# One scaling product for both heads, VectorE sums the pair and GpSimd adds the sum; fewer whole items; filling products in the last waits

## The chip, the cores and the metric

One Trainium2 chip, one of its cores. The metric is device microseconds of one execution; a figure with a range is a median of several. The profile is one execution with the hardware profiler on.

## The reference

Four batches of a 64 x 32 x 32 image pass three stages:

```python
# 1. attention over the 1024 pixels, 32 channels, no mask
q, k, v = wq @ x, wk @ x, wv @ x
x = x + wo @ (softmax(k.T @ q, axis=2) @ v.T).T
t = tokens(x)                                   # (4, 1024, 64)
# 2. causal attention, 8 heads of 64, on layernormed tokens
t = t + concat_h(softmax(mask(q_h @ k_h.T / 8)) @ v_h) @ Wo
# 3. a recurrence over the 1024 tokens, on layernormed tokens
w = batchnorm(layernorm(t) @ W.T) * gamma + beta
y[n] = sigmoid(w[n] + y[n-1] @ V.T);   t = t + y
```

Wo is folded into the value matrices of the heads, so each head's attention gives its own 64-column addend of the tokens.

## The kernel before

Every engine runs its own program; semaphores count finished steps. The middle of all programs is one loop over *slots*, numbered by items, in which each engine does its part of what is listed for that slot.

**Items.** The probabilities are made transposed, in items of 128 keys x 512 queries. The first attention has 64 items, one a slot. The second has 288, in 16 *units* (`v` from `B` on): a unit is one batch and two heads (`r` 0 and 1), nine items for each head, taken in pairs (item of head 0, item of head 1), so nine steps of two slots each. For a pair TensorE multiplies the masks into the banks, then three f16 products per head for the scores (`pe_score_masks`, `pe_scores`). ScalarE reads a bank twice (`act_item`): exponentials in f32 (L775), and again in f16 (L779). GpSimd subtracts the two for the low part (`pool_low`, L1250). Six slots (`LAG`), so three pairs, later TensorE multiplies values (`pe_values`) with f16 high and low parts, three products for each 128 queries (L574, L576, L578). A *whole* item has only the f32 exponentials, no second reading and no low part, and one f32 product for each 128 queries, which the trace shows as two records (L570). `whole(i)` names them: every `ATTN_WHOLE`-th of the 18 items of a unit, so with 6 the 6th, 12th and 18th (pairs 2, 5 and 8, head 1). Item 2's second run of two tiles is multiplied together with item 3.

**The maxima.** In the same slots TensorE computes rough scores of the next unit into two banks (`pe_maxes`, L497, with masks L483) and VectorE reduces each to row maxima (`dve_prep`, L903). TensorE's masks in a slot wait for both maxima of the pair before (`pe_wait_bank`). Each slot's work on TensorE is in this order: values, helpers (`pe_aux`: queries, values, keys), masks of the maxima, masks of the scores, maxima, scores. The masks of the scores wait until ScalarE is done with the first item of the pair before.

**The outputs.** A *half* is one head's output for 512 queries, 4 x 65 columns in a bank; its 65th column is the sum of the exponentials. The halves of head 0 lie in `OT[0]`, those of head 1 in `OT[1]`. The first 512 queries are closed by pair 2, the others by pair 8, each multiplied three pairs later. VectorE then, ahead of its other work in that slot, takes the reciprocals of the four 65th columns and multiplies (`dve_scale`, L979 and L983), into one of four buffers (`S_RING`), head 0 first. GpSimd adds each half to the tokens (`pool_add`, L1260), also ahead of its low parts in that slot. The next half of a head opens its bank only when the half before is scaled. There are 8 halves of the first attention and 64 of the second; the last one is added by VectorE (L1129).

**The tail.** After the loop come layernorm of the last batch (its first half of tokens already inside the loop, L1028 to L1068), transposes (L584), the product with W in two halves (L711), batchnorm statistics with an average over partitions (L715), and the solver: sweeps over four chunks, a product with V on TensorE and a sigmoid on ScalarE.

## Time and profile before

| | |
|---|---|
| median of 3 runs | 570.09 us (568.32 to 572.07) |
| the profiled execution | 568.85 us, span of the trace 567.0 us |
| mean granted TensorE clock | 0.974 |
| TensorE products busy | 490.0 us, 6771 |
| VectorE busy | 398.8 us, 909 |
| ScalarE busy | 429.3 us, 832 |
| GpSimd busy | 424.4 us, 463 |

The span runs from the first to the last instruction of the trace; the profiled execution's time has what lies around it as well. Busy times of TensorE are sums of records that overlap in its pipeline.

### The profile page before, as it was taken

What the parts mean: (1) busy time and instruction counts of PE and PEld (TensorE: products, weight loads), DVE (VectorE), ACT (ScalarE), POOL (GpSimd) and SP (SyncE); (2) the same over time, 40 slices, a digit from 0 to 9 for tenths busy, and PEclk for the clock granted to TensorE, in tenths of its full rate; (3) what the DMA queues carried; (4) which work ended last, traced back from release to release, by engine and by line L of the source; (5) the groups of instructions that cost most, each with busy time, mean ns of one, the idle gap of its engine ahead of it and who ended that gap; (6) DMA issues with size and microseconds to landing.
All of it is one profiled execution on the core that took longest, in us unless ns stands there. A gap on an engine that the chain in (4) does not pass through costs nothing.

```text
span 567.0 us, 16744 instructions
## 1 busy us (share of the span) xinstructions
PE 490.0 (86%) x6771; PEld 323.0 (57%) x6771; DVE 398.8 (70%) x909; ACT 429.3 (76%) x832; POOL 424.4 (75%) x463
## 2 busy tenths in 40 slices
PE   4699978988799998889999988998999999787783
PEld 1277655655565755565666756565666766564431
DVE  5878888767678786576767676766767786328757
ACT  3488867866778878587888878787888878785593
POOL 3867965857988797968788797899788799985002
PEclk9999999989999999799999999999999999998698
DMA  9100000000000000000000000000000000000001
GB/s 230 68 3 2 2 20 1 4 1 3 1 22 2 3 3 2 3 1 21 2 3 2 4 3 1 21 3 1 1 3 3 2 3 2 2 2 2 0 2 74
DMA packets 3580, 7.46 MB, mean 13 GB/s; under 512 B 1168, under 2 KB 1456, under 8 KB 3376
## 3 DMA queue, kind: packets, MB, share of 16 engines
q1 hardware_dynamic: 3056, 5.34, 3.5%
q8 instruction: 54, 0.88, 0.7%
q10 hardware_dynamic: 448, 1.05, 0.6%
q14 instruction: 22, 0.18, 0.1%
HBM read 4.22 MB, written 1.05 MB: 9 GB/s over the span
## 4 chain that ended last, share of the span: by engine, by line
PE 45%; DVE 22%; POOL 17%; ACT 9%; issue 6%; DMA 1%; DVEq 0%; SPq 0%; POOLq 0%; ACTq 0%
POOL probs_low L1250 10%; PE bank L537 9%; DVE attn_partial_max L903 7%; ACT probs_high L779 6%; PE bank L497 6%; PE bank L570 5%; PE bank L574 4%; DVE conv_partial_max L897 3%; PE bank L578 3%; PE bank L576 3%; PE bank L455 2%; PE bank L522 2%; PE bank L483 2%; PE bank L456 2%; POOL tokens L1260 2%
## 5 line engine op out<-in xcount | busy, mean ns | idle before, releaser
L1250 POOL TENSOR_TENSOR probs_low<-probs,probs_high 128x512 f16<-128x512 f32 x288 | 327.6, 1158 | 77.5 <-ACT probs_high L779 76.7
L775 ACT ACTIVATE probs<-bank 128x512 f32<-128x512 f32 x352 | 214.7, 611 | 84.2 <-PE bank L537 69.0
L903 DVE TENSOR_REDUCE attn_partial_max<-bank 128x1 f32<-128x512 f32 (+2 forms) x288 | 185.3, 685 | 99.5 <-PE bank L497 99.0
L779 ACT ACTIVATE probs_high<-bank 128x512 f16<-128x512 f32 x288 | 176.8, 614 | 0.0
L574 PEld LDWEIGHTS bank<-values_high,probs_high 128*128 128x128 f16 x1152 | 105.7, 98 | 74.2 <-issue 35.8
L574 PE MATMUL bank<-values_high,probs_high 128*128 128x65 f16 x1152 | 128.8, 196 | 15.5 <-POOL probs_low L1250 11.4
L576 PE MATMUL bank<-values_low,probs_high 128*128 128x64 f16 x1152 | 127.6, 194 | 0.0
L578 PE MATMUL bank<-values_high,probs_low 128*128 128x65 f16 x1152 | 127.1, 194 | 0.0
L576 PEld LDWEIGHTS bank<-values_low,probs_high 128*128 128x128 f16 x1152 | 106.9, 99 | 3.2
L578 PEld LDWEIGHTS bank<-values_high,probs_low 128*128 128x128 f16 x1152 | 107.2, 98 | 0.0
L570 PE MATMUL bank<-values,probs 128*128 128x65 f32 x512 | 71.7, 278 | 0.8 <-POOL probs_low L1250 0.8
L570 PEld LDWEIGHTS bank<-values,probs 128*128 128x128 f32 x512 | 64.7, 192 | 3.5 <-POOL probs_low L1250 1.0
L497 PE MATMUL bank<-attn_keys_high,queries_high 64*128 64x512 f16 (+3 forms) x384 | 56.7, 332 | 7.9 <-ACT probs_high L779 6.0
L1260 POOL TENSOR_TENSOR tokens<-scaled_outputs,tokens 128x256 f32<-128x256 f32 x71 | 51.7, 729 | 8.0 <-DVE scaled_outputs L983 3.3
L537 PE MATMUL bank<-queries_high,attn_keys_high 64*128 64x512 f16 (+3 forms) x384 | 55.6, 326 | 1.1 <-ACT probs_high L779 1.1
L537 PE MATMUL bank<-queries_high,attn_keys_low 64*128 64x512 f16 (+3 forms) x384 | 55.5, 325 | 0.0
L537 PE MATMUL bank<-queries_low,attn_keys_high 64*128 64x512 f16 (+3 forms) x384 | 55.5, 325 | 0.0
L897 DVE TENSOR_REDUCE conv_partial_max<-bank 128x1 f32<-128x512 f32 x64 | 42.8, 687 | 5.8 <-PE bank L470 4.7
L983 DVE TENSOR_TENSOR scaled_outputs<-bank,reciprocal_denominators 128x256 f32<-128x256 f32 x72 | 30.6, 425 | 7.6 <-DVE reciprocal_denominators L979 0.5
L522 PE MATMUL bank<-causal_masks,identity_bf 128*128 128x128 bf16 x256 | 27.5, 219 | 6.6 <-ACT probs_high L779 6.4
L497 PEld LDWEIGHTS bank<-attn_keys_high,queries_high 64*128 64x128 f16 x384 | 15.3, 93 | 29.7 <-issue 6.8
L1343 POOL TENSOR_TENSOR x_split<-probs 128x512 f32<-128x512 f32 x4 | 4.2, 1092 | 36.1 <-ACT probs L878 36.1
(192 smaller groups left out, 708.9 us busy)
## 6 DMA issues: line engine op xcount, KB each, us to landing
x_channels<-in_x_cm SPq DMA_DIRECT2D x6, 256.0 KB, 7.6
tokens<-in_x_tm SPq DMA_DIRECT2D x1, 1024.0 KB, 10.4
out<-ln_channels SPq DMA_DIRECT2D x4, 256.0 KB, 2.0
attn_weights<-in_attn_w ACTq DMA_DIRECT2D x1, 512.0 KB, 6.2
attn_keys_split<-attn_keys_high SPq DMA_DIRECT2D x4, 128.0 KB, 2.3
attn_keys_split<-attn_keys_low SPq DMA_DIRECT2D x4, 128.0 KB, 2.4
queries_high<-minus_max_rows SPq DMA_DIRECT2D x32, 2.0 KB
x_channels<-in_x_cm ACTq DMA_DIRECT2D x2, 128.0 KB, 3.2
```

Source lines behind the costliest of these rows:

```text
L497: last[r] = nc.tensor.matmul(prep_bank(m + r)[:, at * P:(at + tiles) * P], q[rows(r), t * P:(t + 1) * P], xs_hi[rows(r), b * N + j0 * P:b ...
L537: last[r] = nc.tensor.matmul(ST[(i + r) % ST_RING][:, at * P:(at + tiles) * P], keys[rows(r), b * N + j * P:b * N + (j + 1) * P], queries[ ...
L570: ins = nc.tensor.matmul(dst, e32[:, item % E_RING, cols], v32[v % 2][:, j, r, :], start=opens, stop=True, skip_group_check=True)
L574: nc.tensor.matmul(dst, hi, v_hi[v % 2][:, j, r, :], start=opens, stop=False, skip_group_check=True)
L576: nc.tensor.matmul(dst[:, 0:C], hi, v_lo[v % 2][:, j, r, :], start=False, stop=False, skip_group_check=True)
L578: ins = nc.tensor.matmul(dst, lo, v_hi[v % 2][:, j, r, :], start=False, stop=True, skip_group_check=True)
L775: ins = nc.scalar.activation(e32[:, i % E_RING, :], o[:], ACT.Exp, scale=scale)
L779: ins = nc.scalar.activation(p_hi[:, i % P_RING, :], o[:], ACT.Exp, scale=scale)
L897: nc.vector.reduce_max(cmx[v % 2][:, t, part:part + 1], o[:], AX).then_inc(s_prep_used, 1)
L903: nc.vector.reduce_max(dst, o[:].rearrange("p (n w) -> p n w", n=n), AX).then_inc(s_prep_used, 1)
L1250: nc.gpsimd.tensor_tensor(out=p_lo[:, i % P_RING, :], in0=e32[:, i % E_RING, :], in1=p_hi[:, i % P_RING, :], op=ALU.subtract).then_inc(s_r ...
L1260: nc.gpsimd.tensor_tensor(out=dst, in0=scaled[:, half % S_RING, :, :], in1=dst, op=ALU.add).then_inc(s_added, 1)
```

## The change

- The reciprocals of both heads are taken in one instruction and both outputs are scaled in one product (`dve_scale_pair`), for which the two output banks become one tensor. It waits until both heads' values are closed. VectorE then sums the two scaled outputs, and GpSimd adds the sum to the tokens: one add for a pair, not two. The last pair is added by VectorE.
- `ATTN_WHOLE` goes from 6 to 9, so the whole items of a unit are the 9th and the 18th: head 0 of pair 4, and head 1 of pair 8.
- `pe_keep_clock` puts bf16 products of 256 columns into a bank that nobody reads, in five places behind the loop: 8, 6, 22, 3 and 18 of them.

```diff
-CONV_WHOLE, ATTN_WHOLE = 4, 6
+CONV_WHOLE, ATTN_WHOLE = 4, 9
+def added_by(half):
+    return half + 1 if half < B * NC else B * NC + (half - B * NC) // 2 + 1
-        banks = [ctx.enter_context(nc.psum_tensor(f"bank{i}", [P, CW], f32)) for i in range(8)]
-        ST, MX, OT, AUX = banks[0:3], banks[3:5], banks[5:7], banks[7]
+        banks = [ctx.enter_context(nc.psum_tensor(f"bank{i}", [P, CW], f32)) for i in range(6)]
+        both = ctx.enter_context(nc.psum_tensor("output_banks", [P, 2, CW], f32))
+        ST, MX, OT, AUX = banks[0:3], banks[3:5], (both[:, 0, :], both[:, 1, :]), banks[5]
+        def pe_keep_clock(bank, n):
+            for _ in range(n):
+                nc.tensor.matmul(bank[:, 0:2 * P], identbf[:], masks[:].rearrange("p a c -> p (a c)"),
+                                 start=True, stop=True)
...
             pe.wait_ge(s_l3t, 2)
+            pe_keep_clock(MX[0], 8)
             pe.wait_ge(s_l3, 3)
             pe_transposes(MX[1], xh3, 2).then_inc(s_tr, 1)
+            pe_keep_clock(MX[0], 6)
             pe.wait_ge(s_trc, 1)
             nc.tensor.matmul(ST[0][:], ffn_w[:, 0, :], xh3T[:, 2 * CW:3 * CW], start=True, stop=True).then_inc(s_wxp, 1)
+            pe_keep_clock(MX[0], 22)
             for t in range(TPC):
                 pe.wait_ge(s_l3, 4 + t)
...
             pe.wait_ge(s_aux_used, len(AUXES))
+            pe_keep_clock(ST[1], 3)
...
             pe.wait_ge(s_bn3, 1)
             pe.wait_ge(s_t2c, 2)
+            pe_keep_clock(MX[0], 18)
...
+        def dve_scale_pair(half):
+            nc.vector.wait_ge(s_values, CLOSED_BY[half + 1][3] + 1)
+            i = half % S_RING
+            po = both[:, :, 0:TPC * PO].rearrange("p r (t c) -> p r t c", c=PO)
+            nc.vector.reciprocal(rden[:, i:i + 2, :], po[:, :, :, C:PO].rearrange("p r t c -> p r (t c)")) \
+                .then_inc(s_recip, 2)
+            if half >= S_RING:
+                nc.vector.wait_ge(s_added, added_by(half - S_RING))
+            nc.vector.wait_ge(s_recip, half + 2)
+            nc.vector.tensor_tensor(out=scaled[:, i:i + 2, :, :], in0=po[:, :, :, 0:C],
+                                    in1=rden[:, i:i + 2, :].unsqueeze(3).to_broadcast([P, 2, TPC, C]),
+                                    op=ALU.mult).then_inc(s_scaled, 2)
+            nc.vector.wait_ge(s_scaled, half + 2)
+            nc.vector.tensor_tensor(out=scaled[:, i, :, :], in0=scaled[:, i, :, :], in1=scaled[:, i + 1, :, :],
+                                    op=ALU.add).then_inc(s_paired, 1)
...
                 for half in HALVES_AT.get(g, ()):
-                    dve_scale(half)
+                    if half < B * NC:
+                        dve_scale(half)
+                    elif half % 2 == 0:
+                        dve_scale_pair(half)
...
-            dve.wait_ge(s_added, HALVES - 1)
-            dve.wait_ge(s_scaled, HALVES)
+            dve.wait_ge(s_added, added_by(HALVES - 3))
+            dve.wait_ge(s_paired, (HALVES - B * NC) // 2)
...
-            nc.gpsimd.wait_ge(s_scaled, half + 1)
+            if half < B * NC:
+                nc.gpsimd.wait_ge(s_scaled, half + 1)
+            else:
+                nc.gpsimd.wait_ge(s_paired, (half - B * NC) // 2 + 1)
...
-                    if half < HALVES - 1:
+                    if half < B * NC or half % 2 == 0 and half < HALVES - 2:
                         pool_add(half)
```

## Rows read from the trace of the kernel before

**Rows 1.** The page, its part 4: shares of the chain that ended last.

```profile
PE 45%; DVE 22%; POOL 17%; ACT 9%; issue 6%; DMA 1%; DVEq 0%; SPq 0%; POOLq 0%; ACTq 0%
```

**Rows 2.** Stretches: length, busy time (count) by engine, clock, DMA share, GB/s.

```profile
421.71:445.40 23.69, 22.55 (x356) 15.42 (x356) 17.39 (x40) 19.85 (x39) 19.84 (x20) 1.00 0.01 3
470.00:500.00 30.00, 25.75 (x414) 17.88 (x410) 12.80 (x28) 23.66 (x48) 27.66 (x37) 1.00 0.01 2
524.00:526.00 2.00, 0.33 (x2) 0.18 (x1) 1.73 (x10) 0.60 (x1) 0.00 (x0) 0.50 0.01 4
```

**Rows 3.** Groups by line: busy us, mean ns, idle before and its releaser.

```profile
L1250 POOL TENSOR_TENSOR probs_low<-probs,probs_high 128x512 f16<-128x512 f32 x288 | 327.6, 1158 | 77.5 <-ACT probs_high L779 76.7
...
L1260 POOL TENSOR_TENSOR tokens<-scaled_outputs,tokens 128x256 f32<-128x256 f32 x71 | 51.7, 729 | 8.0 <-DVE scaled_outputs L983 3.3 <-POOL tokens L1260 0.4
...
L983 DVE TENSOR_TENSOR scaled_outputs<-bank,reciprocal_denominators 128x256 f32<-128x256 f32 x72 | 30.6, 425 | 7.6 <-DVE reciprocal_denominators L979 0.5
...
L964 DVE TENSOR_TENSOR queries_low<-bank,queries_high 128x512 f16<-128x512 f32 x32 | 21.8, 681 | 0.0
```

**Rows 4.** Timeline of ScalarE, slot 4: start, length, instruction.

```profile
434.74 0.64 ACT L775 ACTIVATE probs<-bank 128x512 f32<-128x512 f32 x1
435.22 0.65 ACT L779 ACTIVATE probs_high<-bank 128x512 f16<-128x512 f32 x1
```

**Rows 5.** The chain in order of time, slot 6: start, us, what.

```profile
437.62 0.47 PE bank L570 x4
...
438.42 0.03 PE bank L578
438.45 0.26 PE bank L483 x2
```

**Rows 6.** Timeline of VectorE, slots 4 and 5 of the unit.

```profile
435.18 0.68 DVE L964 TENSOR_TENSOR queries_low<-bank,queries_high 128x512 f16<-128x512 f32 x1
435.78 0.17 DVE L979 RECIPROCAL reciprocal_denominators<-bank 128x4 f32<-128x4 f32 x1
436.06 0.42 DVE L983 TENSOR_TENSOR scaled_outputs<-bank,reciprocal_denominators 128x256 f32<-128x256 f32 x1
...
437.01 1.28 DVE L903 TENSOR_REDUCE attn_partial_max<-bank 128x1 f32<-128x512 f32 x2
```

**Rows 7.** Timeline of VectorE, layernorm of the last batch and the last sum.

```profile
513.71 1.08 DVE L988 TENSOR_SCALAR ln_rstd<-ln_var_eps 128x4 int32<-128x4 int32 x1
...
517.05 1.08 DVE L996 SCALAR_TENSOR_TENSOR ln_rstd<-ln_newton_scratch,ln_rstd 128x4 f32<-128x4 f32 x1
518.16 0.17 DVE L994 TENSOR_TENSOR ln_newton_scratch<-ln_rstd,ln_var_eps 128x4 f32<-128x4 f32 x1
...
521.71 0.42 DVE L1129 TENSOR_TENSOR tokens<-scaled_outputs,tokens 128x256 f32<-128x256 f32 x1 [0.22 <-POOL tokens L1260]
```

**Rows 8.** Timeline of GpSimd, the same stretch.

```profile
511.37 6.73 POOL L1250 TENSOR_TENSOR probs_low<-probs,probs_high 128x512 f16<-128x512 f32 x6
```

**Rows 9.** Timeline of GpSimd, slots 3 to 5 of the unit.

```profile
433.50 2.27 POOL L1250 TENSOR_TENSOR probs_low<-probs,probs_high 128x512 f16<-128x512 f32 x2 [0.24 <-ACT probs_high L779]
435.95 2.28 POOL L1250 TENSOR_TENSOR probs_low<-probs,probs_high 128x512 f16<-128x512 f32 x2 [0.17 <-ACT probs_high L779]
```

**Rows 10.** Timeline of VectorE, first reciprocals of slot 5, first and last of 11.

```profile
155.86 0.17 DVE L979 RECIPROCAL reciprocal_denominators<-bank 128x4 f32<-128x4 f32 x1
...
459.84 0.17 DVE L979 RECIPROCAL reciprocal_denominators<-bank 128x4 f32<-128x4 f32 x1
```

**Rows 11.** Timeline of TensorE: one f32 product in the loop, the others in the tail.

```profile
398.29 1.12 PE L660 MATMUL bank<-ln_channels,ffn_weights 128*128 128x512 f32 x2 [0.49 <-DVE values_low L959]
...
522.08 2.07 PE L702 MATMUL bank<-ln_channels,ffn_weights 128*128 128x512 f32 x2 [0.69 <-ACT ln_channels L845]
525.82 1.14 PE L584 MATMUL bank<-constants,ln_tokens 128*128 128x128 f32 x4 [1.67 <-DVE ln_tokens L1135]
527.08 2.04 PE L711 MATMUL bank<-ln_channels,ffn_weights 128*128 128x256 f32 x4
```

More of the change, by code:

```diff
@@ L370, in build @@
         s_scaled = sem("outputs_scaled")
+        s_paired = sem("outputs_of_both_heads_added")
         s_added = sem("outputs_added")
@@ L980, in dve_scale @@
             if half >= S_RING:
-                nc.vector.wait_ge(s_added, half - S_RING + 1)
+                nc.vector.wait_ge(s_added, added_by(half - S_RING))
             nc.vector.wait_ge(s_recip, half + 1)
@@ L1017, in dve_ln3_tile @@
             if first:
-                nc.vector.wait_ge(s_added, (B + (b + 1) * H) * NC)
+                nc.vector.wait_ge(s_added, added_by((B + (b + 1) * H) * NC - 1))
             link(nc.vector.bn_stats(stats3[:, t, :], tok[:, (t * B + b) * C:(t * B + b + 1) * C]))
@@ L1060, in dve_norms @@
             if g == LAST_STATS_SLOT:
-                nc.vector.wait_ge(s_added, half_of(UNITS - 1, 0, 1) + 1)
+                nc.vector.wait_ge(s_added, added_by(half_of(UNITS - 1, 0, 1)))
                 last_stats(0)
@@ L1123, in _ @@
                 dve_norms(g)
-            dve.wait_ge(s_added, HALVES - 1)
-            dve.wait_ge(s_scaled, HALVES)
+            dve.wait_ge(s_added, added_by(HALVES - 3))
+            dve.wait_ge(s_paired, (HALVES - B * NC) // 2)
             dst = tok3[:, TPC:NT, (B - 1) * C:B * C]
-            link(nc.vector.tensor_tensor(out=dst, in0=scaled[:, (HALVES - 1) % S_RING, :, :], in1=dst, op=ALU.add))
+            link(nc.vector.tensor_tensor(out=dst, in0=scaled[:, (HALVES - 2) % S_RING, :, :], in1=dst, op=ALU.add))
             last_stats(1)
@@ L1255, in pool_add @@
             b = batch_of(v)
-            nc.gpsimd.wait_ge(s_scaled, half + 1)
+            if half < B * NC:
+                nc.gpsimd.wait_ge(s_scaled, half + 1)
+            else:
+                nc.gpsimd.wait_ge(s_paired, (half - B * NC) // 2 + 1)
             if half:
-                nc.gpsimd.wait_ge(s_added, half)
+                nc.gpsimd.wait_ge(s_added, added_by(half) - 1)
             dst = tok3[:, c * TPC:(c + 1) * TPC, b * C:(b + 1) * C]
@@ L1333, in _ @@
                     if g == slot + 8:
-                        pool.wait_ge(s_added, (B + (2 + n) * H) * NC)
+                        pool.wait_ge(s_added, added_by((B + (2 + n) * H) * NC - 1))
                 for k in range(NC):
```

## The prediction

> **What bounds the kernel now.** I read the shares of the chain that ended last first, then the groups by cost, then one repeating stretch engine by engine. In the chain no engine leads alone: TensorE has 45% of the span, VectorE 22%, GpSimd 17%, ScalarE 9% [rows 1]. So a saving on one engine is worth nothing until I know who ends the wait in each slot.
>
> The second attention repeats a unit (a batch and two heads) of nine slots of two items each, and from 421.71 to 445.40 us one takes 23.69 us. In it GpSimd is busy 19.84 us and VectorE 17.39; TensorE shows 22.55, but its records overlap, so that is no measure of it [rows 2]. In other stretches GpSimd is the bound: 27.66 us of 30 from 470 to 500 us [rows 2]. The clock is 1.00 in both; in the tail it is at 0.50, the lower of the two levels (1.2 GHz), from 524 to 526 us [rows 2].
>
> I number a unit's slots 0 to 8. The half of the output that closes first in a unit is scaled in slot 5, the other in slot 2 of the next unit.
>
> **GpSimd's work.** Removed: 32 of its 71 adds (39 are left), at 729 ns, 23.3 us. Added: 16 low parts at 1158 ns, 18.5 us, since "whole" items go from 48 to 32 of 288 [rows 3]. Net 4.8 us less in all, 0.3 us a unit. That counts only where GpSimd is the bound, about four units' worth of the run: 1.3 us. Against it stands the new sum of VectorE, below; I take nothing for the two together.
>
> **ScalarE's work.** 16 more exponentials. Two in a row start 0.48 us apart (434.74, 435.22) [rows 4], so 7.7 us in all, mostly in second items of slots 2 and 5, behind which ScalarE waits for scores anyway. In slot 4 the first item becomes whole, which frees the scores of slot 5 by up to 0.48 us. Whether that is worth anything is settled by VectorE (below).
>
> **TensorE's work.** The chain gives 0.47 us for four f32 value products (half of an item's eight), so 0.94 for a whole item, and 0.03 for each f16 product, so 0.36 for a split item's twelve [rows 5]. Each item that is split saves 0.58 us: 9.3 us over 16. But by place it is not a plain saving: per unit slot 8 loses one whole item (0.58 less), slot 7 gains one (0.58 more), and slots 5 and 6 each lose half of one. Slots 7 and 8 are near TensorE's bound both, so they nearly cancel. I take +0.1 us a unit, 1.5 us for 15 units; the bounds are one such item either way, -0.58 and +0.58 us a unit, since either can be hidden while the other is not.
>
> **VectorE's work.** This is the step that decides. Before, two reciprocals and two products run from 435.78 to 437.01, when the first maximum of slot 5 starts: 1.23 us [rows 6]. After: one reciprocal (0.28 to the product's start, 435.78 to 436.06 [rows 6]), one product over 512 columns (681 ns by the 512-column product that reads a bank, L964 [rows 3]), and a sum of two SBUF tiles over 256 columns (0.42 us by the last sum, L1129 [rows 7], of which 0.34 are seen by an instruction that does not need its result: half of the 1.23, less the reciprocal's 0.28). With 0.04 between, 0.28 + 0.68 + 0.04 + 0.34 = 1.34 us, 0.1 more than before.
>
> The sum has a second cost. VectorE instructions on four columns with their inputs in SBUF, 0.17 us when GpSimd is idle (518.16), took 1.08 us four times in a row, from 513.71 to 517.05 [rows 7]. GpSimd meanwhile ran six low parts without a gap from 511.37, 6.73 us, or 1.12 each [rows 8]. The third border lies at 514.74 and the last part ends at 518.10; the first and the fourth of those instructions end at 514.79 and 518.13. So each waited until GpSimd's current instruction was over. The products that read a bank kept their 425 ns on average [rows 3] while GpSimd was busy beside them. The new sum reads two SBUF tiles: it should wait likewise, and then hold GpSimd for up to its own 0.34 us.
>
> The Trainium skill says the same of wider operands (SBUF — State Buffer, section "Who interferes with whom"): a VectorE instruction with two SBUF inputs contends with a GpSimd instruction that reads SBUF, and whoever starts first keeps the other out for its whole length. It speaks against this change; no row here shows a two-input sum of 256 columns beside GpSimd. By that page the wait is the rest of GpSimd's instruction, as I take it; without the page's rule and the small rows the sum would cost 0.1 us.
>
> How long is the wait? In slot 5 the sum is ready at 435.78 + 1.00 = 436.78. GpSimd's turn there: before, it starts a low part at 433.50 and one at 435.95 [rows 9]. After, slot 2's second item gives one low part more, so I work the queue forward at 1.13 us each: slot 3's two end at about 436.3, slot 4's only one starts at about 436.35 (its exponential ends then: 434.74 + 3 x 0.48 plus a semaphore) and ends at 437.5. The sum gets in at 437.5, and slot 5's first maximum starts at about 437.85 instead of 437.01: **0.8 us later**. The bounds are 0.1 us (no wait) and 1.2 (a whole low part and 0.1).
>
> Who is late next? TensorE's masks of slot 6 start at 438.45 right behind the value products [rows 5], and they also wait for both maxima of slot 5, which end at 437.01 + 1.28 = 438.29 [rows 6]. So VectorE is level with TensorE now, and what it is late, slot 6 is late. The earlier scores of slot 5 do not help: VectorE runs without a gap into slot 5, no row from the low queries at 435.18 on has idle time before it [rows 6], and TensorE's shorter values in slot 6 are finished before. What is queued behind the sum on VectorE is the maxima, the row maxima, and layernorm tiles; on GpSimd, the add of the pair waits for the sum, and behind it slot 5's low parts, for which the values come due three slots later, so they have the room.
>
> In how many units? In 11 of the 15 that prepare another, the reciprocal of this half starts without any idle time before it, from 155.86 to 459.84 [rows 10]. Two of them (at 331 and 384 us) lie where the chain, read in pieces of 10 us, is mostly GpSimd's, as such a stretch shows in [rows 2]. Nine units by 0.8 us: **7.2 us**. In slot 2 the sum is ready about 0.3 us before a border, and VectorE has 0.4 us to spare behind it: nothing, but for the slots where the keys of the next batch are transposed; 0.5 us for all. A unit that is longer gives GpSimd time to work off what the layernorms left: I take off 1.0 us.
>
> **The tail.** The last pair is scaled and summed on VectorE with GpSimd idle: 0.1 us more, but the wait for GpSimd's add ahead of the last sum, 0.22 us [rows 7], goes. Nothing. The filling products (57 of 256 columns) are to keep the clock. At 0.50 the f32 product took 2.07 us for two records of 512 columns, at 1.00 1.12 us [rows 11]. On the chain lie the last transposes, 1.14 us, and the Wx products in two halves, 2.04 us [rows 11]; the first half's is covered in part by statistics that VectorE still runs. I give the transposes 0.3, the Wx products 0.8 and the averages 0.1: **1.2 us saved**. The product at 522.08 is off the chain: its result is needed 2 us later. The fillers cost nothing if they end inside the wait: 22 of them at 0.11 us are 2.4 us, between the end of a fast product (about 523.2) and the tokens at 525.6. If the clock were low they would take 0.21 us each, 4.6 from 524.15 on, and end 3 us after the tokens: bounds -1.6 and +3 us. The solver's first sweep at the low clock hides behind ScalarE's sigmoids.
>
> **The sum.** 7.2 + 1.5 + 0.5 - 1.0 - 1.2 + 0 = +7.0 us on the profiled execution's 568.85 (span 567.0 and 1.85 around it), so 575.9; the median of the runs is 1.24 above it, so **577 us**.
>
> **Rivals.**
> *A. The sum does not wait for GpSimd.* The small instructions at 513.71 and after are of another size, and a sum of 256 columns may get in otherwise, or arrive between two low parts. Then slot 6 is late by 0.1 us: 0.9 + 1.5 - 1.2 and 1.3 less for GpSimd's stretches is -0.1: 570 us. For it: no row of this width beside GpSimd. Against: four of four.
> *B. TensorE's saving is on the path and VectorE's lateness is not: faster.* Values are products right behind each other in the chain, and slot 8 is one that TensorE ends. If in 12 units its 0.58 us counts, and slot 7's cost falls in the wait for ScalarE there, the gain is 7.0; with 1.2 from the tail and 1.3 from GpSimd's stretches, 560.6 us. It decides if the pair's sum ends less than about 0.1 us later than the second product does now. Against it stands that VectorE is level already.
> *C. Full price.* The queue moves so that the sum always just misses: 1.2 us x 11, 1.5 and 0.5 us as above, and the tail's fillers at the low clock, +3: 588 us.
> *D. The fillers do not hold the clock* while the rest is as forecast: 577 + 1.2 + 3 = 581 us; inside the range.
>
> **How the numbers follow.** Forecast with D 0.47, A 0.28, B 0.16, C 0.09. The forecast's own range is 572 to 582 (nine units at 0.4 to 1.2 us). The range that should hold 8 in 10 takes in A with its tail bound and part of C: 564 to 585. A change under 1%, 5.7 us, can hardly be told from none here. Slower by over 1%: most of the forecast's cases and C, 0.52. Within 1%: A, the low part of the forecast and of B, 0.31. Faster: 0.17.
>
> **What would show it.** Right: the line of the pair's sum on VectorE with a mean well over 425 ns, often ending where a low part ends; its first maximum in slot 5 later after the reciprocal than 1.23 us; masks waiting for the maxima; units of 24.3 us or more; the clock at 1.00 between 520 and 530 us. Wrong: the sum at 425 ns (A), units under 23.5 us (B), or the masks of slot 6 still released by TensorE's own values, in which case VectorE had room that I did not see.

## The result and the profile after

The changed kernel took **583.6 us**, median of 4 runs (582.11 to 586.57), against 570.31 us for the kernel before on the same chip (568.32 to 572.07): 1.0241 times as long, with a 95% interval of 1.0188 to 1.0293. The profiled execution took 583.34 us, its span is 581.5 us (567.0 before), its mean granted clock 0.979 (0.974 before). The forecast was 577 us in a range of 564 to 585. So the direction and the range held, and the size of the change, +7, was about half of what was measured, +13.3.

The shares of the chain that ended last, to be held against [rows 1]:

```profile
PE 37%; DVE 31%; POOL 15%; ACT 11%; issue 5%; DMA 0%; DVEq 0%; SPq 0%; POOLq 0%; ACTq 0%
```

VectorE has gone from 22% of the span to 31%, TensorE from 45% to 37%. By stretches, with the columns of [rows 2] (a whole unit, the stretch from 470 us, and 2 us of the tail):

```profile
436.42:461.86 25.44, 21.80 (x361) 14.90 (x361) 19.65 (x40) 20.24 (x41) 19.56 (x18) 1.00 0.01 2
470.00:500.00 30.00, 25.55 (x413) 16.90 (x411) 21.92 (x42) 23.39 (x46) 25.58 (x36) 1.00 0.01 3
...
534.00:554.00 20.00, 17.85 (x119) 11.27 (x119) 17.24 (x68) 9.79 (x19) 0.00 (x0) 1.00 0.00 1
```

A steady unit takes 25.44 us, where it took 23.69. VectorE's busy time in it rose by 2.26 us (17.39 to 19.65) though it has one instruction to the pair less; 0.4 us of that is one more layernorm tile that happens to lie in this stretch. The groups by line show where that sits (columns as in [rows 3]):

```profile
L1008 DVE TENSOR_TENSOR scaled_outputs<-scaled_outputs 128x256 f32<-128x256 f32 x32 | 28.7, 897 | 1.1
L1302 POOL TENSOR_TENSOR tokens<-scaled_outputs,tokens 128x256 f32<-128x256 f32 x39 | 28.2, 724 | 8.7 <-DVE scaled_outputs L1008 8.4 <-DVE scaled_outputs L1019 0.3
...
L1004 DVE TENSOR_TENSOR scaled_outputs<-output_banks,reciprocal_denominators 128x512 f32<-128x512 f32 x32 | 22.1, 692 | 4.3
```

The sum of the pair (L1008) shows 897 ns on average, while the same form of instruction, 256 columns from two SBUF tiles, took 0.42 us in [rows 7] with GpSimd idle. The product of 512 columns (L1004) is at 692 ns, as forecast from L964 in [rows 3]. GpSimd is less busy than before, 420.2 us of the span against 424.4, and from 470 to 500 us 25.58 against 27.66 [rows 2], though that stretch now holds somewhat earlier work: it isn't what became the bound.

Who waits for VectorE's maxima now (the view of waits of the kernel after, where L497 is the masks and L511 the rough scores; the columns are us in all, times, longest):

```profile
PEld bank L497 <- DVE attn_partial_max L922: 18.6, 30, 1.4
PE bank L497 <- DVE attn_partial_max L922: 15.2, 28, 1.3
PEld bank L511 <- DVE attn_partial_max L922: 14.2, 14, 1.4
```

The same view of the kernel before, where L483 is the masks and L497 the rough scores:

```profile
PEld bank L497 <- DVE attn_partial_max L903: 6.7, 13, 0.7
...
PE bank L483 <- DVE attn_partial_max L903: 1.4, 6, 0.4
```

Products and weight loads overlap, so the rows of an engine's two parts aren't to be added; but the masks' wait went from 1.4 us to 15.2, and that of the rough scores' weights from 6.7 to 14.2 in about as many places (13 and 14), at most 1.4 us each instead of 0.7.

**By slots.** The start of ScalarE's first exponential of a pair marks the slot. The distances between these starts in one steady unit, and the sum of their differences over units 1 to 15, worked out from ScalarE's timeline (the distance to slot n is put down to slot n; 421.71 is the start of a slot 8 and 436.42 of a slot 0, so both stretches are nine slots long):

```
slot                      0     1     2     3     4     5     6     7     8   unit
before, from 421.71      2.51  2.88  2.95  2.29  2.40  2.26  2.71  2.43  3.26  23.69
after, from 436.42       2.57  2.87  2.96  3.18  2.40  1.95  3.81  2.82  2.88  25.44
units 1 to 15, after
  less before            (0, 1, 2, 4 together +0.7)
                                         +10.0       -3.6  +9.6  +5.7  -7.3
```

Slots 5 and 6 together are +6.0, slots 7 and 8 together -1.6. Unit 0 gives -1.2 and the work ahead of it +0.7. That is +14.8 until the last pair starts (515.05 before, 529.80 after), and the rest of the span is 0.25 us shorter. So two places pay: slot 6, where the sum of slot 5 is in the way, and slot 3, behind the sum of slot 2.

**Slot 5**, as forecast. VectorE's timeline of the kernel after, to be held against [rows 6]:

```profile
423.44 0.20 DVE L999 RECIPROCAL reciprocal_denominators<-output_banks 128x8 f32<-128x8 f32 x1
423.77 0.69 DVE L1004 TENSOR_TENSOR scaled_outputs<-output_banks,reciprocal_denominators 128x512 f32<-128x512 f32 x1
424.50 1.04 DVE L1008 TENSOR_TENSOR scaled_outputs<-scaled_outputs 128x256 f32<-128x256 f32 x1
425.46 1.28 DVE L922 TENSOR_REDUCE attn_partial_max<-bank 128x1 f32<-128x512 f32 x2
```

GpSimd's, to be held against [rows 9]:

```profile
424.10 1.16 POOL L1289 TENSOR_TENSOR probs_low<-probs,probs_high 128x512 f16<-128x512 f32 x1 [0.67 <-ACT probs_high L798]
```

And TensorE's, the masks of slot 6:

```profile
426.88 0.27 PE L497 MATMUL bank<-causal_masks,identity_bf 128*128 128x128 bf16 x2 [1.02 <-DVE attn_partial_max L922]
```

The low part occupies GpSimd from 424.10 to 425.26, and the sum, started at 424.50, ends 0.28 us after it. The first maximum follows 2.02 us after the reciprocal (forecast 2.07; 1.23 before). TensorE's masks of slot 6 come behind the maxima, after 1.02 us of idle time.

**Slot 2**, not as forecast. VectorE's timeline of the kernel after, 17 us later:

```profile
440.58 0.21 DVE L999 RECIPROCAL reciprocal_denominators<-output_banks 128x8 f32<-128x8 f32 x1 [0.23 <-PE output_banks L584]
440.93 0.69 DVE L1004 TENSOR_TENSOR scaled_outputs<-output_banks,reciprocal_denominators 128x512 f32<-128x512 f32 x1
441.65 1.42 DVE L1008 TENSOR_TENSOR scaled_outputs<-scaled_outputs 128x256 f32<-128x256 f32 x1
443.00 1.28 DVE L922 TENSOR_REDUCE attn_partial_max<-bank 128x1 f32<-128x512 f32 x2
```

GpSimd's:

```profile
440.52 2.27 POOL L1289 TENSOR_TENSOR probs_low<-probs,probs_high 128x512 f16<-128x512 f32 x2 [0.67 <-ACT probs_high L798]
```

And TensorE's weight load of the rough scores of slot 3:

```profile
444.34 0.12 PEld L511 LDWEIGHTS bank<-attn_keys_high,queries_high 64*128 64x128 f16 x2 [1.41 <-DVE attn_partial_max L922]
```

GpSimd runs two low parts without a gap from 440.52 to 442.79; the border between them lies near 441.65. The sum is ready at 441.65, does not get in there, and takes 1.42 us, 1.0 us more than its own work of 0.42: nearly a whole low part. The weight load comes 0.06 us behind the maxima. For comparison the same place on VectorE in the kernel before:

```profile
428.07 0.17 DVE L979 RECIPROCAL reciprocal_denominators<-bank 128x4 f32<-128x4 f32 x1
...
429.40 1.29 DVE L903 TENSOR_REDUCE attn_partial_max<-bank 128x1 f32<-128x512 f32 x2
```

and on ScalarE, the second exponential of slot 2:

```profile
430.55 0.59 ACT L779 ACTIVATE probs_high<-bank 128x512 f16<-128x512 f32 x1
```

Measured from the first exponential of slot 2 (430.05 before, 442.25 after, so 12.20 us apart) the maxima start 1.40 us later: 443.00 - 12.20 = 430.80 against 429.40. Before, they had room: the rough scores of slot 3 waited for the exponential that ends at 431.14, 0.45 us after the maxima do (430.69). Of the 1.40 us, 0.95 are left, and slot 3 is 0.89 longer (2.29 to 3.18). The sums of slot 2 are longer than 0.5 us in 12 of 15 units, 1.01 us on average: 1.42 us in five units, 1.14 in three, 0.68 to 0.91 in four, and 0.42 or 0.43 in the other three. So to just miss a border, as here, is the dearest case but not the only one; in seven units the sum is ready somewhere in the middle of a low part and waits for the rest of it.

**The tail.** VectorE, to be held against [rows 7]:

```profile
532.36 1.08 DVE L1030 TENSOR_TENSOR ln_newton_scratch<-ln_rstd,ln_var_eps 128x4 f32<-128x4 f32 x1
533.47 0.17 DVE L1031 SCALAR_TENSOR_TENSOR ln_newton_scratch<-ln_newton_scratch,ln_rstd 128x4 f32<-128x4 f32 x1
...
536.35 0.42 DVE L1008 TENSOR_TENSOR scaled_outputs<-scaled_outputs 128x256 f32<-128x256 f32 x1
536.88 0.42 DVE L1168 TENSOR_TENSOR tokens<-scaled_outputs,tokens 128x256 f32<-128x256 f32 x1
```

TensorE, to be held against [rows 11]:

```profile
536.92 1.13 PE L718 MATMUL bank<-ln_channels,ffn_weights 128*128 128x512 f32 x2
537.88 2.56 PE L460 MATMUL bank<-causal_masks,identity_bf 128*128 128x256 bf16 x22
540.99 0.55 PE L598 MATMUL bank<-constants,ln_tokens 128*128 128x128 f32 x2 [0.54 <-DVE ln_tokens L1174]
```

With GpSimd idle from 533.42 on, the last sum takes 0.42 us and the small instructions fall from 1.08 to 0.17. The 22 filling products end at 540.44, 0.55 us before the transposes are ready, and the clock is 1.00 from 534 to 554 us where it was 0.50 from 524 to 526 [rows 2]. From the last sum of tokens to the first sigmoid of the solver it is 10.48 us (536.88 to 547.36), before 11.79 (521.71 to 533.50).

### The profile page after: what moved, and what is told of

Same layout as the page of the kernel before. It is cut to its first block, busy times and chain, and to the rows that moved or that the text cites. A ratio compares the mean times of both kernels' runs of the same rounds, so it can differ in the third digit from the quotient of the medians.

```text
span 581.5 us, 16912 instructions
## 1 busy us (share of the span) xinstructions
PE 482.5 (83%) x6892; PEld 316.9 (54%) x6892; DVE 424.4 (73%) x877; ACT 436.0 (75%) x848; POOL 420.2 (72%) x447
## 4 chain that ended last, share of the span: by engine, by line
PE 37%; DVE 31%; POOL 15%; ACT 11%; issue 5%; DMA 0%; DVEq 0%; SPq 0%; POOLq 0%; ACTq 0%
DVE attn_partial_max L922 10%; POOL probs_low L1289 10%; PE bank L551 7%; ACT probs_high L798 5%; PE bank L511 5%; PE output_banks L584 4%; DVE conv_partial_max L916 3%; PE output_banks L588 3%; ACT probs L794 3%; DVE scaled_outputs L1008 3%; DVE scaled_outputs L1004 2%; PE output_banks L592 2%; PE bank L469 2%; PE output_banks L590 2%; DVE queries_low L983 2%
## 5 line engine op out<-in xcount | busy, mean ns | idle before, releaser
L588 PEld LDWEIGHTS output_banks<-values_high,probs_high 128*128 128x128 f16 x1216 | 111.7, 98 | 71.4 <-POOL probs_low L1289 35.6
L588 PE MATMUL output_banks<-values_high,probs_high 128*128 128x65 f16 x1216 | 133.1, 196 | 18.8 <-POOL probs_low L1289 9.4
L590 PE MATMUL output_banks<-values_low,probs_high 128*128 128x64 f16 x1216 | 132.1, 194 | 0.0
L592 PE MATMUL output_banks<-values_high,probs_low 128*128 128x65 f16 x1216 | 131.7, 194 | 0.0
L590 PEld LDWEIGHTS output_banks<-values_low,probs_high 128*128 128x128 f16 x1216 | 112.6, 99 | 3.5 <-issue 0.6
L592 PEld LDWEIGHTS output_banks<-values_high,probs_low 128*128 128x128 f16 x1216 | 112.8, 98 | 0.0
L511 PE MATMUL bank<-attn_keys_high,queries_high 64*128 64x512 f16 (+3 forms) x376 | 56.6, 331 | 12.5 <-ACT probs_high L798 8.6
L584 PEld LDWEIGHTS output_banks<-values,probs 128*128 128x128 f32 x384 | 47.6, 191 | 9.2 <-issue 6.8
L584 PE MATMUL output_banks<-values,probs 128*128 128x65 f32 x384 | 51.4, 277 | 0.0
L497 PE MATMUL bank<-causal_masks,identity_bf 128*128 128x128 bf16 x251 | 27.0, 218 | 15.2 <-DVE attn_partial_max L922 15.2
L536 PE MATMUL bank<-causal_masks,identity_bf 128*128 128x128 bf16 x256 | 27.4, 219 | 9.5 <-ACT probs_high L798 9.5
L1302 POOL TENSOR_TENSOR tokens<-scaled_outputs,tokens 128x256 f32<-128x256 f32 x39 | 28.2, 724 | 8.7 <-DVE scaled_outputs L1008 8.4
L511 PEld LDWEIGHTS bank<-attn_keys_high,queries_high 64*128 64x128 f16 x376 | 15.3, 93 | 33.3 <-DVE attn_partial_max L922 14.2
```

Source lines behind the costliest of these rows:

```text
L511: last[r] = nc.tensor.matmul(prep_bank(m + r)[:, at * P:(at + tiles) * P], q[rows(r), t * P:(t + 1) * P], xs_hi[rows(r), b * N + j0 * P:b ...
L584: ins = nc.tensor.matmul(dst, e32[:, item % E_RING, cols], v32[v % 2][:, j, r, :], start=opens, stop=True, skip_group_check=True)
L588: nc.tensor.matmul(dst, hi, v_hi[v % 2][:, j, r, :], start=opens, stop=False, skip_group_check=True)
L590: nc.tensor.matmul(dst[:, 0:C], hi, v_lo[v % 2][:, j, r, :], start=False, stop=False, skip_group_check=True)
L592: ins = nc.tensor.matmul(dst, lo, v_hi[v % 2][:, j, r, :], start=False, stop=True, skip_group_check=True)
L1302: nc.gpsimd.tensor_tensor(out=dst, in0=scaled[:, half % S_RING, :, :], in1=dst, op=ALU.add).then_inc(s_added, 1)
```

## The experiments

Each ratio is that to the kernel before, run on the same chip, with its 95% interval.

**e1, the pair without the other two parts.** The kernel after with

```diff
-CONV_WHOLE, ATTN_WHOLE = 4, 9
+CONV_WHOLE, ATTN_WHOLE = 4, 6
-            pe_keep_clock(...)      # all five calls
...
```

> The change with ATTN_WHOLE back at 6 and without the filling products: one product for both heads, the sum on VectorE, one add on GpSimd. Theory (the sum of two SBUF tiles waits for the low part that GpSimd has in hand, in slot 2 for a whole one, in slot 5 for a part of one, and the maxima behind it come late): 578 to 586 us, the sum's line at 750 ns or more on average, no gain from the whole items. Rival W (the shift of the whole items and their f32 products on TensorE is what costs): at most 572 us. Rival J (it is the waiting for both heads and the joint product, not the sum): 578 us or more too, but with the sum at 425 ns.

Measured: 581.83 us, 1.0209 (1.0184 to 1.0235). The pair alone gives nearly the whole loss, and the sum's line shows 869 ns, which speaks for the sum and against the mere joint product. In a steady unit slots 3 and 6 are 3.18 and 3.01 us instead of 2.29 and 2.71, the others as before.

**e2, the whole items alone.** The kernel before with `ATTN_WHOLE` 9.

> The kernel before with ATTN_WHOLE at 9 and nothing else: 16 more low parts on GpSimd with all 71 adds. Theory: TensorE saves in slot 8 what it loses in slot 7, GpSimd has 18 us more to do and is the bound in more places: 570 to 577 us. Rival W: 578 us or more.

Measured: 573.84 us, 1.0072 (1.0045 to 1.0099), +4.1 us. The shares of its chain:

```profile
PE 36%; POOL 24%; DVE 23%; ACT 11%; issue 5%; DMA 1%; DVEq 0%; POOLq 0%; SPq 0%; ACTq 0%
```

and of its waits that of GpSimd for ScalarE:

```profile
POOL probs_low L1250 <- ACT probs_high L779: 65.5, 69, 2.6
```

GpSimd's part of the chain goes from 17% to 24% and it waits 65.5 us for ScalarE where it waited 76.7 [rows 3]. So sixteen low parts more, without the adds saved, do cost: GpSimd gets near the bound.

**e3, the filling products alone.** The kernel before with the 57 products in the same five places.

> The kernel before with the 57 filling products of the tail and nothing else. Forecast of the prediction: 1.2 us less, 568.9 us, with the clock at 1.00 from the last values to the first sweep; 1.31 us less from the last sum of tokens to the first sigmoid, if the trace of the changed kernel is a guide. Rival: they delay what is behind them, 570.1 us or more.

Measured: 567.79 us, 0.9972 (0.9952 to 0.9992): -1.6 us. The three parts measured alone, 2.09 + 0.72 - 0.28 = 2.53%, agree with the 2.41% of the whole change, so there is no large share that only their combination makes.

**e4, one product for both heads and no sum.** The kernel before with `dve_scale_pair` up to the product and both scaled outputs added by GpSimd as before:

```diff
+            nc.vector.wait_ge(s_values, CLOSED_BY[half + 1][3] + 1)
...
+            nc.vector.reciprocal(rden[:, i:i + 2, :], ...).then_inc(s_recip, 2)
...
+            nc.vector.tensor_tensor(out=scaled[:, i:i + 2, :, :], in0=po[:, :, :, 0:C], ...,
+                                    op=ALU.mult).then_inc(s_scaled, 2)
```

> The kernel before with one reciprocal and one product for both heads, and no sum: GpSimd adds each head's output as before. Theory: the two-input sum is what costs, so this stays within 2 us of before: 568 to 572 us. Rival J (the joint product, its wait for both heads and the later opening of the banks): 575 us or more.

Measured: 569.59 us, 1.0002 (0.9985 to 1.0019). The common wait for both heads, the common reciprocal and the product of 512 columns cost nothing together. What is left of e1 is the sum.

**e5 and e6, VectorE time with two and with one SBUF input.** The kernel before, with one instruction more behind the second product of each pair; nobody reads its result:

```diff
+            if half >= B * NC and half % 2:
+                nc.vector.tensor_tensor(out=spare[:], in0=cst[:, 0:256], in1=cst[:, 256:512], op=ALU.add)   # e5
+                nc.vector.reduce_max(spare[:, 0:1], cst[:, 0:256], AX)                                    # e6
...
+            dve.wait_ge(s_cst, 16)                                                                    # both
```

The last line makes VectorE wait for the constants before its first cast of the run. That starts at 6.86 us (e6) and 6.70 us (e5), in the kernel before at 2.81, and ScalarE's first exponential comes at 25.43 and 25.07 us, where it comes at 22.67 in the kernel before and between 21.5 and 23.6 in all other kernels here.

> The kernel before, and behind each pair's second product a sum of two constant SBUF tiles of 256 columns that nobody reads. Theory (it waits for GpSimd): its line well over 425 ns on average, 550 or more, and 574 to 582 us. Rival (VectorE's own time is the cost, no wait): 425 ns and the time of the kernel with a maximum in its place.

> As the one before, with a maximum over one SBUF tile of 256 columns in the place of the sum: the same time on VectorE, one SBUF input. Theory: no wait, a line of some 425 ns, 571 to 575 us, and less than with the sum.

Measured: e5 587.44 us, 1.0300 (1.0262 to 1.0338); e6 578.63 us, 1.0148 (1.0110 to 1.0186). Both are slower than expected; the later start is part of it. The added instruction among the groups of e5:

```profile
L988 DVE TENSOR_TENSOR spare<-constants 128x256 f32<-128x256 f32 x32 | 24.3, 760 | 0.0
```

and of e6:

```profile
L988 DVE TENSOR_REDUCE spare<-constants 128x1 f32<-128x256 f32 x32 | 13.1, 409 | 0.0
```

In length the two are alike where GpSimd does not bear on them, 0.41 us. The one with two SBUF inputs took 760 ns on average, the other 409, and the kernels differ by 8.8 us. This separates two prices. The 8.8 us are those of the waits on GpSimd; the later start is in both kernels and drops out. Of e6's own 8.4 us (1.48%) the later start takes part: by ScalarE's timeline units 1 to 15 are 6.2 us longer, so the 30 pieces of VectorE work in them cost about 0.2 us each. The two instructions also differ in what they write, 256 columns and one; the products L983 write 256 columns too, with one SBUF input, and keep their 425 ns [rows 3], so it is the second input that costs. In the changed kernel the reciprocal and the product that are saved pay for most of the first (1.07 us to the sum's start and 0.34 for the sum, against 1.23), and the second is left. In e5 a sum that gets in at once looks like this on VectorE:

```profile
311.89 0.45 DVE L988 TENSOR_TENSOR spare<-constants 128x256 f32<-128x256 f32 x1
...
319.60 0.41 DVE L988 TENSOR_TENSOR spare<-constants 128x256 f32<-128x256 f32 x1
```

with GpSimd beside it:

```profile
307.96 2.27 POOL L1254 TENSOR_TENSOR probs_low<-probs,probs_high 128x512 f16<-128x512 f32 x2 [1.35 <-ACT probs_high L780]
310.90 2.45 POOL L1254 TENSOR_TENSOR probs_low<-probs,probs_high 128x512 f16<-128x512 f32 x2 [0.67 <-ACT probs_high L780]
...
318.54 2.50 POOL L1254 TENSOR_TENSOR probs_low<-probs,probs_high 128x512 f16<-128x512 f32 x2 [0.18 <-ACT probs_high L780]
```

and one that just misses, in the same kernel:

```profile
475.53 1.41 DVE L988 TENSOR_TENSOR spare<-constants 128x256 f32<-128x256 f32 x1
```

Two low parts in a row took 2.27 us without a sum and 2.45 and 2.50 with one between them: GpSimd is held for 0.2 us, VectorE in the other case for 1.0 us, nearly a whole low part.

**e7, the sum behind the maxima.** The kernel after; the sum is issued when the maxima of its slot are done, ahead of the low queries:

```diff
+        def dve_sum_pair(half):
+            i = half % S_RING
             nc.vector.wait_ge(s_scaled, half + 2)
             nc.vector.tensor_tensor(out=scaled[:, i, :, :], in0=scaled[:, i, :, :], in1=scaled[:, i + 1, :, :],
                                     op=ALU.add).then_inc(s_paired, 1)
...
                     for m in ms:
                         dve_prep(m)
+                for half in HALVES_AT.get(g, ()):
+                    if half >= B * NC and half % 2 == 0:
+                        dve_sum_pair(half)
```

> The changed kernel with the sum moved behind the slot's two maxima on VectorE. Theory: the maxima, for which TensorE waits, are on time again, and slots 3 and 6 get back most of what they lost; what is left is the wait that now stands ahead of the low queries and the next slot's maxima: 571 to 579 us. Rival (the lateness of the maxima is not what makes slots 3 and 6 longer): 582 us or more.

Measured: **563.68 us, 0.9888 (0.9839 to 0.9937)**, faster than both kernels, and faster than the 571 to 579 us expected. All the work of the change is in it; only one instruction stands two places later in VectorE's queue. The shares of its chain:

```profile
PE 36%; DVE 24%; POOL 23%; ACT 11%; issue 5%; DMA 1%; DVEq 0%; SPq 0%; POOLq 0%; ACTq 0%
```

the sum among its groups:

```profile
L1011 DVE TENSOR_TENSOR scaled_outputs<-scaled_outputs 128x256 f32<-128x256 f32 x32 | 17.7, 552 | 0.1
```

and VectorE's timeline in slots 2 and 5:

```profile
425.79 0.21 DVE L999 RECIPROCAL reciprocal_denominators<-output_banks 128x8 f32<-128x8 f32 x1 [0.23 <-PE output_banks L584]
...
426.80 1.29 DVE L922 TENSOR_REDUCE attn_partial_max<-bank 128x1 f32<-128x512 f32 x2
428.01 0.42 DVE L1011 TENSOR_TENSOR scaled_outputs<-scaled_outputs 128x256 f32<-128x256 f32 x1
...
435.32 0.42 DVE L1011 TENSOR_TENSOR scaled_outputs<-scaled_outputs 128x256 f32<-128x256 f32 x1
```

The maxima start 1.01 us after the reciprocal of slot 2, not 2.42, and the steady unit is 23.47 us (421.62 to 445.09), with slot 3 at 2.29 and slot 6 at 2.73 us. The masks wait 4.1 us in all for the maxima, where it was 15.2:

```profile
PE bank L497 <- DVE attn_partial_max L922: 4.1, 11, 0.4
```

Here the reciprocal waits for TensorE as in the kernel after (0.23 us) and slot 2 has the same four exponentials; slot 3 is still as short as before. So neither the common wait nor the item that is no longer whole made slot 3 long. At 428.01 and 435.32 the low parts had ended and GpSimd was waiting for the sum, so the sum of 0.42 us finds no one in its way. In 8 of the 32 places it still takes 0.68 to 1.17 us (hence the mean of 552 ns), but the slot's maxima no longer stand behind it. GpSimd's adds come later and wait 18.8 us for the sum (8.4 in the kernel after); they have that room.

**e8, the sum taken from the bank.** The kernel after, where head 0 is scaled alone and head 1 is multiplied and added in four instructions of 64 columns, each with one input in the bank and one in SBUF:

```diff
...
+            for t in range(TPC):
+                ins = nc.vector.scalar_tensor_tensor(out=scaled[:, i, t, :], in0=po[:, 1, t, 0:C],
+                                                     scalar=rden[:, i + 1, t:t + 1], in1=scaled[:, i + 1, t, :],
+                                                     op0=ALU.mult, op1=ALU.add)
...
```

> The changed kernel with the same result made another way: head 0's product as before the change, then for head 1 four instructions of 64 columns that multiply the bank by the reciprocal and add head 0's tile, so that each has one SBUF tensor as input. Theory: no wait for GpSimd, VectorE some 0.3 us longer than before the change in slots 2 and 5: 570 to 577 us. Rival (waiting for both heads, or the sum's mere place ahead of the maxima): 580 us or more.

Measured: 573.29 us, 1.0061 (1.0036 to 1.0086). The four instructions among its groups:

```profile
L1009 DVE SCALAR_TENSOR_TENSOR scaled_outputs<-output_banks,reciprocal_denominators,scaled_outputs 128x64 f32<-128x64 f32 x128 | 27.5, 278 | 1.1
```

and in slot 2 on VectorE's timeline:

```profile
432.89 0.21 DVE L999 RECIPROCAL reciprocal_denominators<-output_banks 128x8 f32<-128x8 f32 x1 [0.23 <-PE output_banks L584]
...
433.67 0.86 DVE L1009 SCALAR_TENSOR_TENSOR scaled_outputs<-output_banks,reciprocal_denominators,scaled_outputs 128x64 f32<-128x64 f32 x4
434.44 1.28 DVE L922 TENSOR_REDUCE attn_partial_max<-bank 128x1 f32<-128x512 f32 x2
```

The four together take 0.86 us and don't wait for GpSimd (all 128 of them in the run lie between 273 and 285 ns), and the maxima start 1.55 us after the reciprocal where it was 1.33 before in this slot and 2.42 in the kernel after. With a sum that does not have to wait, three quarters of the loss are gone though the order is kept; the 0.2 to 0.3 us by which VectorE's work here is longer than before are the likely rest, by the price of e6, and that isn't shown by a run of its own.

**e9, the sum later still**, behind the low queries and values of its slot as well.

> The changed kernel with the sum still further back, behind the slot's maxima and behind the subtraction of the low queries. Theory: only what stands ahead of TensorE's next need matters, and the maxima are already ahead of the sum; the low queries are not waited for at once, so this gives 562 to 567 us, within 0.5% of the sum behind the maxima; GpSimd's add and its low parts come 0.6 us later in slot 2. Rival (every instruction further back is worth as much again): 560 us or less.

Measured: 565.97 us, 0.9931 (0.9907 to 0.9954). GpSimd's adds wait 26.0 us now. No better than e7; the intervals overlap, so that it is worse isn't shown.

**e10, e7 with `ATTN_WHOLE` 6.**

> The changed kernel with the sum behind the maxima and ATTN_WHOLE at 6, so 48 whole items again. Alone the 9 cost 0.7%, with GpSimd the engine of 24% of the chain; if that loss is GpSimd's and still there, this is 560 us or less. If the shorter values on TensorE and ScalarE's free slot 4 now count because VectorE is on time, this is slower than with 9: 566 us or more. The theory expects the two to be near each other, 560 to 567 us: GpSimd is 18 us richer and TensorE 9 us poorer.

Measured: 565.84 us, 0.9936 (0.9913 to 0.9959), with TensorE at 49% of the chain, VectorE at 20% and GpSimd at 15%. The intervals of e7 and e10 overlap. So whole items by nine cost 0.7% in the kernel before (e2) and nothing that can be told here, where GpSimd has 32 adds less.

## Why the prediction was right in kind and wrong in size

**The mechanism held.** That the new sum waits for GpSimd's current instruction and delays the maxima was the forecast, and e4, e5, e6 and e7 show it: without the sum nothing is lost, with one of the same length and one SBUF input at most half as much, with the sum behind the maxima the kernel is faster than the one before. Rival A (the sum does not wait) fell to the 897 ns of L1008, rival B (TensorE's saving counts and VectorE's lateness doesn't) to the unit of 25.44 us, rival D to the clock of 1.00 in the tail.

**The terms, in the order of the sum.** The differences of the slots to the kernel before, over units 1 to 15, worked out in the same way from ScalarE's timelines of three more kernels, say what belongs to what:

```
slots                                      3    5 and 6   7 and 8
the kernel after                       +10.0       +6.0      -1.6
e1, the pair alone                      +8.9       +5.6      -1.5
e2, the whole items alone               +0.8       +2.3      +0.1
e7, the sum behind the maxima           +0.9       -3.8      -2.3
```

- *Slot 5's sum, forecast 7.2 us.* Measured +6.0 for slots 5 and 6 together, and in the steady unit +0.79, forecast 0.8. The first maximum 2.02 us after the reciprocal was forecast as 2.07. Against e7, which has all of the change but the sum's place, the two slots are 9.9 us longer, so the sum's place costs more than the net shows.
- *TensorE's values in slots 7 and 8, forecast +1.5.* e2, with the whole items shifted and nothing else, gives +5.5 in slot 7 and -5.4 in slot 8, so they cancel as argued, to +0.1. The -1.6 of the kernel after is not from there: e1, without the shift, has -1.5. What gives it stays open.
- *Slot 2's sum, forecast 0.5 us.* Measured **+10.0**. This is the step that failed: "In slot 2 the sum is ready about 0.3 us before a border, and VectorE has 0.4 us to spare behind it: nothing". The spare time was right (0.45 us). The margin was not: the reciprocal of both heads waits for head 1's values, which in this slot are f32 products (L584), and starts 0.31 us later against ScalarE's first exponential (440.58 - 12.20 = 428.38, before 428.07); and from the reciprocal to the sum's start it is 1.07 us, not 1.00. Together 0.38 us, more than the 0.3 that I had, and all of the margin that there was: the kernel before runs two low parts from 428.32 for 2.27 us, which puts their border near 429.45, 0.38 after 428.07 + 1.00. I worked out the moment from the kernel before as if the first reciprocal kept its place, though in this slot it is released by the first head alone. A loss of a whole low part that hangs on 0.3 us of margin is no term to set to nothing; it is two cases, 0 and about 0.9 us by 11 units, and the second was missing (measured, slot 3 is 0.59 to 0.90 us longer in 12 of the 15 units). Nor does one unit stand for all: in seven of them the sum comes in the middle of a low part. Rival C had it only for slot 5.
- *GpSimd works off its backlog in longer units, forecast -1.0.* No row shows this by itself. The unattributed differences are +0.7 (slots 0, 1, 2 and 4), -1.2 (unit 0) and +0.7 (ahead of it); whether it exists stays open.
- *GpSimd's net work, forecast -4.8 us busy and nothing for the sum.* Measured -4.2 us busy. e2 shows that its price depends on what else GpSimd has to do: +4.1 us when the adds stay.
- *The tail, forecast -1.2 us.* From the last sum to the first sigmoid it is -1.31 us, but 0.64 of that is lost again behind it (see *Open*). e3 alone gives -1.6 us.

With slot 2 at 10.0 the forecast would have been +16.5, and with slots 7 and 8 as measured +13.4; the measured change is +13.3 in the medians and +14.5 in the spans. That this comes so near is partly luck: the backlog's -1.0 is shown by nothing, and slot 5's term was 1.2 too large. The time lies inside the range of 564 to 585 because the range was wide, not because slot 2 had a place in it.

**Who keeps whom out.** The sum of the pair takes up to 1.42 us beside GpSimd, the reduction of one SBUF tile in e6 keeps its 409 ns, and so does the product that reads a bank (425 ns in [rows 3]). The Trainium skill (SBUF — State Buffer, section "Who interferes with whom") has the rule for this: two SBUF inputs contend with a GpSimd instruction that reads SBUF, at most one does not, as long as VectorE isn't in one of its two-port performance modes, and the first to start keeps the other out for its whole length. With that rule the runs here agree on who waits for whom. One input is not always free, though. L988 of the kernel before, a TENSOR_SCALAR with one SBUF input of four columns, took 1.08 us beside the low parts [rows 7] and 0.17 with GpSimd idle:

```profile
523.43 0.17 DVE L988 TENSOR_SCALAR ln_rstd<-ln_var_eps 128x4 int32<-128x4 int32 x1
```

On the length the two sides differ: VectorE is kept out for up to 1.0 us, nearly a whole low part, while a low part behind a sum of 0.42 us is only about 0.2 longer (1.33 to 1.39 us against 1.15 to 1.16 in e5). Whether a part of the 0.42 lies ahead of the moment at which the low part would have read is not shown.

**Open.** From the first sigmoid to the end of the span it is 34.14 us in the kernel after and 33.50 before, and the kernel with the filling products alone has 34.24. So half of what the fillers bring ahead of it is not in the run's time. The traces show where it goes: the granted clock was 0.50, the lower of the two levels (1.2 GHz), in the last sweeps,

```profile
567.00:570.00 3.00, 3.00 (x5) 0.91 (x6) 1.70 (x3) 2.76 (x5) 0.00 (x0) 0.50 0.00 0
```

where the kernel before had 1.00 from 538 to 561 us. Two products of 512 columns took 1.21 us there, one in the kernel before 0.39, and ScalarE's wait for the steps behind them went from 1.09 to 1.58 us. Ahead of it TensorE had run one such product every 0.6 us in both kernels. The fillers need not be the cause: e2, which has none, shows 0.50 from 557.3 to 560.3 us, as far behind its first sigmoid (20 us). Why the clock fell in some kernels and not in others is not shown.

## What to carry to other kernels

Put a VectorE instruction with two SBUF inputs behind whatever the other engines are waiting for, not ahead of it: with GpSimd running long instructions back to back, its length is its own plus up to one of GpSimd's, and here one line moved two places made 583.6 us (1.0241 of the kernel before) into 563.7 (0.9888). Before setting such a step to nothing because it "just gets in", work out how late the step can become and price the case in which it just misses. And if a change takes two waits into one, take the later of the two as the start of everything behind it.

## What of the hardware was not expected

- A VectorE sum that finds GpSimd between two instructions gets in at once (0.41 and 0.45 us in e5) and lengthens GpSimd's pair of low parts by 0.18 to 0.23 us, less than its own length. The other way round the price is 1.0 us.
- Four scalar_tensor_tensor instructions of 64 columns, one input in a bank and one in SBUF with the scalar in SBUF too, took 0.86 us together beside a busy GpSimd (e8): the scalar does not make them wait.
- A TENSOR_SCALAR of four columns with one SBUF input took 1.08 us beside the low parts and 0.17 with GpSimd idle (L988 of the kernel before): here one input was enough to be kept out.
- The reciprocal of 8 columns with a stride over two banks took 204 ns, that of 4 columns 175 ns.
- A piece of VectorE work of 0.41 us in the place of the sum costs about 0.2 us of the run each time (e6, units 1 to 15), though VectorE is busy for 70% of the span only (398.8 us of 567.0).
